# 16-head attentions on one core: row maxima from bfloat16 copies with one product over all keys of a tile, and score steps in two halves of two row groups into two banks each

## The reference, cut to what matters

```python
# L2_attn ("l2a" in the kernel): he = 8; the strictly lower triangle multiplies the scores
xh = x.reshape(b, c, h, he).transpose(0, 2, 1, 3)
q, k, v = jnp.split(jnp.einsum('bhce,ef->bhcf', xh, Wqkv) + bqkv, 3, axis=-1)
att = jnp.einsum('bhqe,bhke->bhqk', q, k) / jnp.sqrt(jnp.float32(he))
mask = jnp.tril(jnp.ones((c, c), dtype=att.dtype), k=-1)
att = jax.nn.softmax(att * mask, axis=-1)
out = jnp.einsum('bhqk,bhke->bhqe', att, v)
# L2_ffn's attention ("l2r"): a latent of 64, HD = 4, rotated q and k, causal with -inf
c = h @ w_down
q = _rope(split(c @ wq), pos); k = _rope(split(c @ wk), pos); v = split(c @ wv)
scores = jnp.einsum('bhqd,bhkd->bhqk', q, k) / jnp.sqrt(jnp.float32(HD))
attn = jax.nn.softmax(jnp.where(causal, scores, -jnp.inf), axis=-1)
```

## Time and profile before

| | us |
|---|---|
| median of 3 runs | 3696.27 |
| the runs | 3695.82 to 3705.57 |
| span of the profiled execution | 3714.3 |
| TensorE busy | 2972.4 (80%) |
| VectorE busy | 2362.2 (64%) |
| ScalarE busy | 1568.7 (42%) |
| GpSimd busy | 773.5 (21%) |

### The profile page before, as it was taken

One profiled execution on the slowest core, in us unless ns is written; L12 is line 12 of the kernel. 1 busy time (PEld: TensorE's weight loads), 2 busy tenths in 40 slices (PEclk: granted clock), 3 DMA queues, 4 the chain that ended last, 5 costly groups with the idle time before them and its releaser, 6 DMA issues. The chain is left out here.

```text
span 3714.3 us, 89913 instructions
## 1 busy us (share of the span) xinstructions
PE 2972.4 (80%) x35888; PEld 2017.2 (54%) x35888; DVE 2362.2 (64%) x6687; ACT 1568.7 (42%) x3160; POOL 773.5 (21%) x823
## 2 busy tenths in 40 slices
PE   3768888689876788868986778876998688798996
PEld 2635556556554455556654445655655354475654
DVE  7575755665777466566677646646667776565457
ACT  4144534434344453534443544353444354344432
POOL 4121312121113121222111322132111122112101
PEclk8679999689987899969998889986999798999998
DMA  1011100000001100000000110000010101000000
GB/s 41 1 36 33 23 7 3 2 2 19 18 1 46 34 19 7 3 2 3 23 14 1 52 31 16 8 2 1 4 31 6 33 21 37 7 3 3 20 18 7
DMA packets 64209, 59.21 MB, mean 16 GB/s; under 512 B 16371, under 2 KB 53156, under 8 KB 63782
## 3 DMA queue, kind: packets, MB, share of 16 engines
q1 hardware_dynamic: 62550, 52.72, 5.2%
q10 hardware_dynamic: 1232, 0.61, 0.1%
HBM read 35.76 MB, written 2.10 MB: 10 GB/s over the span
## 5 line engine op out<-in xcount | busy, mean ns | idle before, releaser
L1333 POOL TENSOR_TENSOR l1t_ss<-l1t_ss,neghalf 128x16 f32<-128x16 f32 x48 | 182.4, 3799 | 333.2 <-DVE l1t_ss L1367 333.2
L256 ACT ACT_TABLE_LOAD x64 | 82.1, 1283 | 304.7 <-PEq L1677 106.5
L2260 ACT ACTIVATE l2r_P<-l2r_bank_score 128x512 f32<-128x512 f32 x240 | 130.3, 594 | 137.2 <-PE l2r_bank_score L1982 137.2
L2260 ACT ACTIVATE l2a_P<-l2a_bank_score 128x512 f32<-128x512 f32 x240 | 130.3, 594 | 131.5 <-PE l2a_bank_score L1982 131.5
L1544 PE MATMUL l1t_ring<-l1f_qkv,x_normT 128*128 128x512 f32 x288 | 162.5, 693 | 12.2 <-ACT x_normT L1238 12.2
L191 POOL TENSOR_TENSOR ln_y_rstd<-ln_var_eps,neghalf 128x4 f32<-128x4 f32 x52 | 52.8, 1015 | 546.5 <-DVE ln_var_eps L212 510.6
L2152 DVE CUSTOM_DVE_ANT_0 l2r_masked<-l2r_bank_ring,l2r_neg_wide 128x512 bf16<-128x512 f32 (+1 forms) x192 | 111.5, 622 | 57.5 <-PE l2r_bank_ring L1951 57.2
L2152 DVE CUSTOM_DVE_ANT_0 l2a_masked<-l2a_bank_ring,l2a_neg_wide 128x512 bf16<-128x512 f32 (+1 forms) x192 | 111.7, 622 | 56.0 <-PE l2a_bank_ring L1951 55.1
L1951 PE MATMUL l2r_bank_ring<-l2r_k_head,l2r_q_head 32*128 32x128 f32 x1824 | 131.6, 285 | 14.9 <-DVE l2r_m L2152 7.4
L1982 PE MATMUL l2a_bank_score<-l2a_q_head,l2a_k_head 32*128 32x128 f32 x1920 | 141.8, 285 | 1.8 <-DMA l2a_q_head<-l2a_shiftT 0.8
L1951 PE MATMUL l2a_bank_ring<-l2a_k_head,l2a_q_head 32*128 32x128 f32 x1824 | 133.1, 287 | 12.2 <-DVE l2a_m L2152 5.3
(11 more groups left out here) (1197 smaller groups left out, 8454.5 us busy)
## 6 DMA issues: line engine op xcount, KB each, us to landing
l1t_v_low<-l1t_v SPq DMA_DIRECT2D x84, 130.0 KB, 2.3
l2x_w<-in_L_ffn_w SPq DMA_DIRECT2D x72, 128.0 KB, 2.3
l1f_qkv<-in_L_ffn_wqkv SPq DMA_DIRECT2D x6, 768.0 KB, 4.3
l1t_v_low_last<-l1t_v_last SPq DMA_DIRECT2D x28, 130.0 KB, 2.3
l1f_tables<-in_l_tables SPq DMA_DIRECT2D x6, 512.0 KB, 5.7
l2e_w_last<-in_L_ffn_w SPq DMA_DIRECT2D x24, 128.0 KB, 2.2
x_in<-in_L_attn_hidden_states SPq DMA_DIRECT2D x8, 256.0 KB, 3.0
out<-x_res SPq DMA_DIRECT2D x8, 256.0 KB, 2.6
```

Source lines behind the costliest of these rows:

```text
L256: act.activation(b.warm[:, column:column + 1], b.neghalf[:, 0:1], func)
L1333: pool.tensor_tensor(ss[:, n % 2], ss[:, n % 2], b.neghalf[:, 0:2 * H8], ALU.pow).then_inc(s["rn_ready"], 1)
L2260: act.activation(self.P[:, use % self.P_RING].rearrange("k h q -> k (h q)"), self.score_bank(h, g)[:, :], ACT.Exp, scale=self.scale).then_ ...
```

## The change

1. **Copies in bfloat16.** New tiles `q_bf` and `k_bf`. GpSimd rounds each 128x512 query tile as it is written (`pool_round`, eight casts an attention); ScalarE signals each query tile for itself. VectorE makes `k_bf`: in l2a from the projection, all heads together with a bias of their own (`bk_all`), in l2r from the key tile.
2. **Maxima.** A unit's head is now one bfloat16 product over all keys of its tile (128 to 512 columns; `pe_max_head`), no longer a float32 product for each key block. Units stand by themselves (`pe_maxima`), not beside scores.
3. **Scores.** Four score banks, one for each row group, and three ring banks. A half is still two row groups.
4. **Order.** A step on TensorE: scores of groups 0 and 1; turns; the first part of the step's units; values of groups 0 and 1 of the step before; scores of groups 2 and 3; second part; values of groups 2 and 3 of the step before; third part. `spread_maxima` deals out 8 units in step 0, 6 in steps 1 to 4, 5 (`AHEAD`) in steps 5 to 13, 3 in step 14; a tile's shift is a turn of the step behind its last unit. ScalarE does the exponentials of two banks, then the turns' copies, then the other two. After the last step the values of both halves come first, then the output's projections, which stood between them.
5. **Set-up of l2a.** VectorE makes both `k_bf`, then the first sequence's keys, the four reductions of tile 0, and then the second sequence's keys. TensorE's maxima of tile 1 wait for both sequences' keys. In l2r the copies to `k_bf` stand behind each key tile.

The diff, cut:

```diff
-    RING, BANKS, P_RING, PV_LAG, KICK = 4, 3, 8, 2, 6
+    RING, P_RING, KICK, AHEAD = 3, 8, 6, 5
...
+        self.q_bf, self.k_bf = sb("q_bf", [128, PAIR, 4, S], BF16), sb("k_bf", [128, PAIR, S], BF16)
...
     def spread_maxima(self):
...
+        left = [(n, g, u) for n in range(2, len(self.tiles))
+                for u in range(0, 4, self.PER_BANK[self.tiles[n][0]]) for g in range(4)]
+        due = [self.first[n] - 2 for n in range(len(self.tiles))]
+        for k in range(len(self.steps)):
+            late = [-(-sum(m <= n for m, _, _ in left) // (due[n] + 1 - k)) for n in range(2, len(due)) if due[n] >= k]
+            count = min(len(left), max(late + [self.AHEAD]))
+            ends = (min(2, count), min(2, count) + (count - min(2, count) + 1) // 2, count)
...
-    def pe_max_piece(self, pe, i, view, r, done):
+    def pe_max_head(self, pe, i, view, c, done):
...
+            ins = pe.matmul(view[:, c, :], self.q_bf[rows, p, u + c, j * 128:(j + 1) * 128],
+                            self.k_bf[rows, p, 0:(j + 1) * 128], start=hb == 1, stop=True, skip_group_check=True)
...
     def pe_first_max(self, pe, n):
...
+        pe.wait_ge(s["q_rounded"], 4 * (n + 1))
+        pe.wait_ge(s["k_rounded"], n + 1)
+        if n:
+            pe.wait_ge(s["k_heads"], PAIR)
...
+    def pe_maxima(self, pe, units):
+
+        while units:
+            some = units[0:2] if self.PER_BANK[self.tiles[self.seq[units[0]][0]][0]] > 1 else units[0:1]
+            units = units[len(some):]
+            views = [self.max_view(i, self.claim(pe, "max", i)) for i in some]
+            for i, view in zip(some, views):
+                self.pe_max_mask(pe, i, view)
+            for c in range(2):
+                for i, view in zip(some, views):
+                    self.pe_max_head(pe, i, view, c, self.s["slot_psum"])
+
+    def pe_scores(self, pe, k, groups):
...
+        if k:
+            pe.wait_ge(s["p_ready"], 4 * k - 3 + groups[-1])
+        for u in range(4):
+            for g in groups:
+                rows = slice(32 * g, 32 * g + 32)
+                ins = pe.matmul(self.s_bank[g][:, u * 128:(u + 1) * 128], self.k[rows, p, self.key_copy(u), keys],
+                                self.q[rows, p, u, queries], start=u == 0, stop=True, skip_group_check=True)
...
     def pe(self, pe, project):
...
+        for k in range(len(self.turn_at)):
+            units = self.units[k] if k < len(self.steps) else ([], [], [])
+            if k < len(self.steps):
+                self.pe_scores(pe, k, (0, 1))
+            for kind, key, _, _ in self.turn_at[k]:
+                turn[kind](pe, key)
+            self.pe_maxima(pe, units[0])
+            if 0 < k <= len(self.steps):
+                self.pe_values(pe, k - 1, (0, 1))
+            if k < len(self.steps):
+                self.pe_scores(pe, k, (2, 3))
+            self.pe_maxima(pe, units[1])
+            if 0 < k <= len(self.steps):
+                self.pe_values(pe, k - 1, (2, 3))
+            self.pe_maxima(pe, units[2])
+            if k == len(self.steps):
+                pe.wait_ge(s["p_ready"], 4 * k)
                 project(pe, 0, self.ORDER)
                 project(pe, 1, self.ORDER[:-1])
...
+    def pool_round(self, pool):
+
+        for p in range(PAIR):
+            for u in range(4):
+                pool.wait_ge(self.s["q_heads"], 4 * p + u + 1)
+                pool.tensor_copy(self.q_bf[:, p, u, :], self.q[:, p, u, :]).then_inc(self.s["q_rounded"], 1)
...
             for p in range(PAIR):
                 dve.wait_ge(s["k_psum"], p + 1)
-                at.dve_keys(dve, p, k_ps[p][:, :], w["head"], w["bk"])
+                dve.tensor_scalar(at.k_bf[:, p, :], k_ps[p][:, :], w["bk_all"][:, 0:1], None, ALU.add)\
+                    .then_inc(s["k_rounded"], 1)
+            at.dve_keys(dve, 0, k_ps[0][:, :], w["head"], w["bk"])
+            at.dve_max(dve, range(4))
+            at.dve_keys(dve, 1, k_ps[1][:, :], w["head"], w["bk"])
             at.dve_first(dve, D)
```

More of the change, by code:

```diff
@@ L1836, in __init__ @@
         self.oT = sb("oT", [self.rows, PAIR, S])
-        self.s_bank = [bank(f"score{i}") for i in range(self.BANKS)]
+        self.s_bank = [bank(f"score{i}") for i in range(4)]
         self.ring = [bank(f"ring{i}") for i in range(self.RING)]
@@ L1867, in count @@
             self.place("v", p, "v_ready", p + 2)
-        for h in range(len(self.turn_at)):
-            if h < self.halves:
-                for i in self.beside[h] + self.extra[h]:
+        for k in range(len(self.turn_at)):
+            for turn in self.turn_at[k]:
+                self.place(*turn)
+            for part in self.units[k] if k < len(self.steps) else ():
+                for i in part:
                     self.place("max", i, "max_ready", i + 1)
-            for turn in self.turn_at[h]:
-                self.place(*turn)
@@ new lines, in spread_maxima @@
+        due = [self.first[n] - 2 for n in range(len(self.tiles))]
[3 more added lines that the diff above has]
+            ends = (min(2, count), min(2, count) + (count - min(2, count) + 1) // 2, count)
+            for c in range(count):
+                part = next(i for i in range(3) if c < ends[i])
+                n = left[0][0]
+                self.units[k][part].append(len(self.seq))
+                self.seq.append(left.pop(0))
```

189 lines of the change are left out of this document (65 added, 124 removed).

## The result

The changed kernel takes 4124.18 us (median of 4 runs, 4114.81 to 4149.91) against 3700.92 us before (4 runs); the ratio is 1.115, 95% interval 1.111 to 1.119. Forecast were 3711.5 us and a range up to 3758.

A forecast was written before the change was run, and what follows sets the result against it. TensorE was taken to set the time, in small steps. Per pass -1.5 + 4.5 + 2.1 - 2.0 + 0.7 = +3.8 us; four passes, +15.2, on 3696.3 gave 3711.5 us, range 3674 to 3758.

The forecast's parts named there:

- The clock falls inside the loop: Rival: two waits of 1 us or more an attention, 2.1 us each, 34 us in all: 3745 us; chance 0.07.
- 1.4 us ahead of tile 5: Loop: wait for the shift's rows ahead of tile 5's first score, 1.4 us.
- the 0.6 of step 5: Loop: wait at step 5, a ring bank being held by a shift until two exponentials are done, 0.6 us.
- The pieces beside scores "are free now": Loop before: maxima's pieces beside scores, on the other row groups, cost nothing; only an extra pair counts, 1.09 us.
- The loop at full clock: Loop's change per attention: l2a -19.4 + 12.9 + 5.0 = -1.5 us, l2r -2.0 us.
- A pair of maxima: Loop: a part of two units on two row groups costs 0.22 us for 512 keys.
- The set-up of l2a: Ahead of l2a's loop: shift 4.5 us later, plus 2.1 us for 4.1 us at half speed.
- the wait for the second keys: Set-up of l2a: TensorE idle 5.8 us until VectorE has written the second keys; the clock then falls.
- The set-up of l2r and the rounding on GpSimd: Ahead of l2r's loop: key copies and last queries' rounding (0.64) delay maxima by 1.3, products give 0.6 back: +0.7 us.
- Parts dearer: Rival: float32/bfloat16 changes cost 0.10 us a part, 3741 us, or units don't run side by side, 3768; chance 0.12.
- The end: After the last step: projections wait for the last values, the chain to the last projection stays: 0.

The follow-up runs named there:

- scores computed twice: Changed kernel, but the first half of a step computes all four row groups' scores, those of groups 2 and 3 for nothing: 3833.8 us, 1.036 of before.
- the maxima alone: Kernel before with bfloat16 copies and one product over all keys a unit, ahead of the half's scores; old banks and order: 3884.2 us profiled, 3981.6 in the other.
- the run with six of them: Changed kernel with six warm-up products at each of the six steps that hold a shift: 3816.7 us, 1.032 of before.
- the run with the warmed set-up and slow l2a loops: Kernel before with bfloat16 maxima ahead of scores and warm-up products in l2r's loop waits and the set-up's waits: 3896.2 us, 1.053 of before.
- the last run: Changed kernel with scores over four row groups at once, old key order, warm-up products in set-up and before tile 0's shift, six units a step: 3667.6 us, 0.990.

## Why the prediction was wrong

- **The step that failed** is the price of the rival "The clock falls inside the loop": "the grant is half as long as in the earlier trace rows, 2.1 us each"; the sum itself has no term for it. The waits were foreseen in the main: 1.4 us ahead of tile 5 was measured as 1.37 to 1.41 where the loop got there at full clock, the 0.6 of step 5 as 0.97, and 0.93 came for VectorE's maxima in the first two steps. But a fall did not cost 2.1 us. In the earlier trace rows the grant came back behind ten bfloat16 products over all rows; in the changed kernel's loops it did so behind the suffix products alone, and the later falls lasted to the loop's end: 103 us in three l2a, 64 in the last, some 136 in three l2r, where they come at the second step, and the whole loop in the second l2r. The loops cost +361 us, where the rival had 34. Its condition was off too: it asks for waits of 1 us or more, and most of the falls came behind 0.93 to 0.97. The prediction also gave it a chance of 0.07, from one idle time of 1.16 us without a fall. The kernel before itself spoke otherwise: the window at 570 us above, a fall in a loop that a different mix of work ended.
- **The pieces beside scores "are free now".** Right for the time at full clock, but they did something else: they kept all four row groups in use. That use had no price in the sum. That it is what ended the falls of the kernel before is argued from the runs with scores computed twice and with the maxima alone, and wasn't shown in that kernel itself.
- **The loop at full clock**: forecast -1.5 (l2a) and -2.0 (l2r); less the kicks the run with six of them has -0.5 and 0.0, some stretches at half clock included. A pair of maxima cost what was forecast: from the scores over it to the values are 1.00 + 0.31 us, and 1.09 without it, so 0.22.
- **The set-up of l2a**: the wait for the second keys 5.74 us (forecast 5.8), the grant 0.50 behind it: both right. Its length was not: 13 us, from 523.8 to the warm-up products, instead of 4.1. So 25.0 us against 15.1: +9.9 instead of +6.6, 40 us in four passes.
- **The set-up of l2r and the rounding on GpSimd**: eight casts took 5.23 us, 0.65 each, as taken (0.64). But they stand in a queue, and the sum counted the last one alone: TensorE waited 1.84 us for them in the first l2a and 3.29 in the first l2r, and the grant fell behind the second of these. An l2r's set-up cost +4.0 us instead of +0.7, 16 in four passes; all else outside the loops gave some 7 us back.
- The Trainium skill, "GPSIMD Engine Reference", section 3.1, has 768 ns as a best case for 512 elements; the casts' row, 0.65 us each, is below that, so the measurement decides.
- **Parts dearer**: no drain between float32 scores and bfloat16 maxima can be seen; the maxima, on row groups like the scores, start 1.00 us after the scores' start, the values, over all rows, 1.09 to 1.11.
- The Trainium skill, "TensorEngine Tiling (Array Packing)", Key Properties, has a drain at a change of tiling mode only; the trace agrees.
- **The end** and the order of the projections weren't measured apart; they are part of the 7 us above.

The Trainium skill, "TensorE: Matmul & The Clock Gate", Part 1, has it that activity of TensorE releases the throttle. The rows qualify that: busy 66.66 of 67 us and 103.69 of 105 at a grant of 0.50. What TensorE does while busy counts, by the run that computes scores twice.

What stays open: what exactly counts. Products on all four row groups brought the clock back here, bfloat16 products over all rows mostly as well; six of these did not in the set-up of the changed kernel's second l2r, and the value projections of an l2a's set-up, float32 products of one row and of all rows in turn, did not in 8 us. Rows, type, number and pauses of products weren't tried one by one. Nor is it known which wait a fall follows: one of 0.71 us was followed by a fall in one kernel, those of 1.39 and 1.41 us were not in another, and the same l2a loop without an edit held in two runs and fell in the third.

## What to carry to other kernels

Ask of each wait that a change adds not only how long it is, but what the granted clock does behind it and which work would bring it back; a loop that fills half of TensorE's rows may run for its whole length at half speed after one wait of a microsecond. Work beside other products that looks free may be what keeps the clock up, so look at the grant at full and at low level before taking it away. Where a wait can't go, a few full products into a bank that is overwritten anyway can fill it at little cost; they guard that wait alone, as the run with the warmed set-up and slow l2a loops shows.

## What the runs showed of the hardware

Both levels of the clock occur under the same work: the last steps of a loop, scores and values without maxima, ran at 1.00 in the kernel before (at 620 us) and at 0.50 in the changed one (at 675), with TensorE busy 4.51 and 5.00 of 5 us. Behind a fall the loops with two row groups at a time mostly kept the low level to their end, but not always: four low stretches in two runs ended after 34 to 37.5 us. That 16 score products on two row groups take as long (1.16 us) as 32 on four (1.17, the last row of the last run) was put to use for the scores themselves: with the new maxima an l2a's loop became 9 us shorter than in the kernel before, and the new maxima alone gave 7.
